# A wait on the previous group's landing ahead of each group's indirect returns

## The reference

```python
gates = softmax(xf @ router_w)
top_v, top_i = top_k(gates, 2)
masked = zeros_like(gates).at[arange(N)[:, None], top_i].set(top_v)
masked = masked / (masked.sum(-1, keepdims=True) + 1e-9)
# _ffn: h = x * rsqrt(mean(x*x) + eps) * rw; silu(h @ W1) @ W2   (128 -> 256 -> 128)
routed = vmap(lambda rw, W1, W2: _ffn(xf, rw, W1, W2))(rms_w, w1, w2)
routed_out = einsum('end,ne->nd', routed, masked)
return layernorm(x + routed_out + shared)
```

## Time and profile before

| | busy us | share of the span | instructions |
|---|---|---|---|
| TensorE matmul | 651.3 | 85% | 4299 |
| TensorE weight load | 554.7 | 72% | 4299 |
| VectorE | 596.1 | 77% | 1744 |
| ScalarE | 444.7 | 58% | 1225 |
| GpSimd | 501.3 | 65% | 545 |

### The profile page before, as it was taken

How to read it: one execution, slowest core, us unless ns; L and a number is a source line. 1 busy time by engine, 2 the same in 40 slices (tenths; PEclk the granted TensorE clock), 3 DMA queues, 4 the chain that set the end, 5 groups by cost and what they waited for, 6 DMA issues and landing times.

```text
span 769.2 us, 14716 instructions
## 1 busy us (share of the span) xinstructions
PE 651.3 (85%) x4299; PEld 554.7 (72%) x4299; DVE 596.1 (77%) x1744; ACT 444.7 (58%) x1225; POOL 501.3 (65%) x545
## 2 busy tenths in 40 slices
PE   5987798999999999999999997965988878767830
PEld 4765576788888888888888886854987768656720
DVE  4999999999999999999999864427447343698875
ACT  4885688867877876787787543411223111346445
POOL 1144565887797897888888776556655656566561
PEclk9999999999999999999999998878889889997865
DMA  8541111211221121111111055114222236536126
GB/s 305 193 138 42 43 43 41 64 57 55 62 64 62 60 62 50 63 64 60 59 50 62 22 167 192 45 55 101 80 80 77 76 80 172 168 100 205 60 80 218
DMA packets 62638, 70.76 MB, mean 92 GB/s; under 512 B 10335, under 2 KB 45285, under 8 KB 62304
## 3 DMA queue, kind: packets, MB, share of 16 engines
q1 hardware_dynamic: 41568, 47.70, 19.6%
q0 software_dynamic: 8608, 16.87, 6.5%
q10 hardware_dynamic: 12384, 5.26, 2.9%
HBM read 48.55 MB, written 23.01 MB: 93 GB/s over the span
## 4 chain that ended last, share of the span: by engine, by line
PE 60%; DVE 13%; issue 12%; ACT 7%; another core or an unknown queue 4%; ACTq 2%; DMA 1%; DVEq 0%; SPq 0%
PE bank L745 7%; PE bank L817 6%; PE bank L826 6%; PE bank L884 6%; PE bank L770 5%; PE bank L800 5%; DVE xbcT_area L1155 3%; PE bank L881 3%; PE bank L871 3%; PE bank L833 3%; PE bank L785 3%; PE bank L888 2%; DVE decay_area L1163 2%; ACT x L933 2%
## 5 line engine op out<-in xcount | busy, mean ns | idle before, releaser
L623 POOL DMA_INDIRECT returned<-xT,slots_in x141 | 142.1, 1008 | 107.6 <-DVE xT L1453 67.3
L669 POOL DMA_INDIRECT dispatched<-rows,row_u x128 | 143.7, 1123 | 33.9 <-issue 31.8
L745 PE MATMUL bank<-xT 128*128 128x128 f32 x564 | 92.0, 316 | 43.4 <-issue 24.9
L1155 DVE SCALAR_TENSOR_TENSOR xbcT_area<-raw,conv_w,xbcT_area 128x512 f32<-128x512 f32 x162 | 123.9, 766 | 2.9 <-ACT xbcT_area L999 2.9
L745 PEld LDWEIGHTS bank<-xT 128*128 128x128 f32 x564 | 82.7, 226 | 50.7 <-issue 42.4
L944 ACT ACTIVATE raw<-bank 128x512 f32<-128x512 f32 (+1 forms) x71 | 39.8, 590 | 126.9 <-remote 61.5
L661 POOL TENSOR_TENSOR state_kept<-state,whole 128x256 f32<-128x256 f32 x56 | 72.1, 1288 | 59.0 <-DVE state L1181 49.1
L1453 DVE COPY xT<-bank 128x512 f32<-128x512 f32 (+1 forms) x36 | 24.3, 676 | 90.5 <-remote 72.8
L770 PE MATMUL bank<-xbcT_area,raw 128*128 x564 | 83.4, 308 | 4.7 <-issue 4.6
L1163 DVE TENSOR_TENSOR_SCAN decay_area<-decay_area,ident_heads 128x512 f32<-128x512 f32 x64 | 85.0, 1329 | 0.0
L770 PEld LDWEIGHTS bank<-xbcT_area,raw 128*128 128x128 f32 x564 | 79.6, 224 | 7.0 <-issue 7.0
(11 more groups left out here) (228 smaller groups left out, 1497.0 us busy)
## 6 DMA issues: line engine op xcount, KB each, us to landing
decay_area<-decay_rows SPq DMA_DIRECT2D x64, 256.0 KB
slots_in<-dispatched ACTq DMA_DIRECT2D x77, 64.5 KB
hid<-returned SPq DMA_DIRECT2D x18, 256.0 KB
slots_in<-dispatched SPq DMA_DIRECT2D x64, 64.5 KB
xT<-xT_dram SPq DMA_DIRECT2D x8, 512.0 KB, 7.9
x<-x_dram SPq DMA_DIRECT2D x8, 512.0 KB, 7.8
out_dram<-x SPq DMA_DIRECT2D x16, 256.0 KB
xT<-returned SPq DMA_DIRECT2D x14, 256.0 KB
```

The costliest lines, as they stand in the source:

```text
L623: e.indirect_dma_start(returned, bass.IndirectOffsetOnAxis(ap=slots_in[sb_][:, n, D:ROW].bitcast(U32), axis=0), slots_out[b][:, n * P:(n + ...
L669: e.indirect_dma_start(dispatched, bass.IndirectOffsetOnAxis(ap=row_u[t % 2][:, m:m + 1], axis=0), rows[t % 3][:, k, c4, :], None).then_in ...
L745: mm = e.matmul(bank[:, off:off + P], w1_now[b][:, k * P:(k + 1) * P], slotsT[gr % len(slotsT)][:, n % 4 * P:(n % 4 + 1) * P], start=True, ...
L1155: e.scalar_tensor_tensor(o, r[:, n:n + W], conv_w[:, k, TAPS - 1 - n:TAPS - n], o, ALU.mult, ALU.add).then_inc(S["conv"])
```

## The change

In `return_rows`, GpSimd waits, for every group but the first, until the four returns of the group ahead of it have landed, before it issues its own. The group ahead has b = (gr - 1) % 3, and is the ((gr - 1) // 3 + 1)th to count on that semaphore. Nothing else is changed.

```diff
@@ -619,6 +619,8 @@
                 b, sb_ = gr % len(slots_out), gr % len(slots_in)
                 on.wait_ge("routed_out", gr + 1)
                 on.wait_ge(f"slots_in{sb_}", 16 * tiles_upto(gr, len(slots_in)))
+                if gr > 0:
+                    on.wait_ge(f"returned{(gr - 1) % len(slots_out)}", 64 * ((gr - 1) // len(slots_out) + 1))
                 for n in range(len(slot_tiles(gr))):
                     e.indirect_dma_start(returned, bass.IndirectOffsetOnAxis(ap=slots_in[sb_][:, n, D:ROW].bitcast(U32), axis=0),
                                          slots_out[b][:, n * P:(n + 1) * P], None, bounds_check=NOWHERE - 1,
```

## The result

The changed kernel takes 774.74 us (median of 4 runs, 772.85 to 776.12) where the kernel before takes 719.05. The ratio is 1.077, with a 95% interval of 1.074 to 1.080: 56 us slower. 748.6 us was predicted, in a range of 723 to 764. The direction and the mechanism were right, the size was not: 28 us of loss were forecast, half of what was measured.

What follows compares the result with a forecast made beforehand. In timed runs GpSimd's issue was taken to bound the middle, with each wait exposing a landing and a restart. Start of group 4 517.3, 31 periods of 6.82 us 211.4 and the end 19.9 gave 748.6 us, range 723 to 764.

Steps and rivals of the forecast that it cites:

- the sum: Changed kernel's timed run: group 4's start 517.3, 31 periods to group 35 211.4, the end 19.9; 748.6 us.
- the holds of TensorE: Routed part: TensorE's signals held about 5 us in the middle, 22.0 us together ahead of it; taken as absent in timed runs.
- the check of it: Kernel before, summed without the 22.0 us of holds: 517.3, 102, 75 and 19.9 give 714, near 720.5 us.
- The rival with real holds: Routed part: TensorE's holds occur in timed runs too, pace already near the floor; 722 to 734 us, chance 0.23.
- faster: Middle: the wait cuts runs of eight returns into fours and TensorE's hold goes; 709 us, chance 0.05.
- no effect: Returns: the wait never ends last, as the group ahead has always landed; 720 us, chance 0.04.
- groups 1 to 3 pay nothing: Ahead of the middle: groups 1 to 3 stand apart by far more than the gap, so the wait costs them nothing.
- The price of one wait: Between two groups on GpSimd: landing 1.25 plus restart 0.77, a gap of at least 2.02 us (1.9 to 2.4).
- TensorE's clock: Routed part: a slower middle may lower it further; priced at nothing, or a few us if VectorE's copy doesn't lead.
- a rival of 2.2 us throughout: Returns: landings of 2.2 us or more under load, period 7.8; 778 us, chance 0.06.
- The split between profile and timed runs: Span grows little, from 769.2 to 770 or 785, while timed runs grow by 28 us.
- Nothing behind GpSimd hides it: Routed part: three result buffers let VectorE run ahead, but what GpSimd can't issue is not made up for.

Runs made afterwards that it cites:

- the second profile: The kernel before, unchanged, profiled once more: 718.83 us, with a span of 717.1 us.
- the leaner TensorE: The kernel before with half of TensorE's products that make a group's result left out: 718.84 us, ratio 1.001.
- the first profile: The profile of the kernel before shown ahead of the prediction: a span of 769.2 us.
- a quarter of the picks' bytes: The changed kernel with only a quarter of the bytes of each of SyncE's picks fetched, same number of DMAs and waits: 766.59 us, ratio 1.067.
- the wait in the middle only: The kernel before with the wait of the change for groups 1 to 23 only: 756.62 us, ratio 1.053.
- the run with dead work: The kernel before with two dead GpSimd multiplications ahead of each group but the first, in place of the wait for a landing: 752.12 us, ratio 1.046.

## Why the prediction was right and wrong

**The step that failed** is the sum, 517.3 + 211.4 + 19.9, in two of its terms; the cost that it is built on, a landing and a restart in every group, was right. The start of group 4 was taken as 517.3 us, with nothing paid by groups 1 to 3, and is 526.66. The period was taken as 6.82 us for all 31 groups and is 7.36, most of it because some landings are slow.

**What bounds the kernel.** The reading that the holds of TensorE were absent in timed runs, and that GpSimd's issue is the pace there, was the step I was least sure of. It held: the second profile has no holds and 5.18 us per group for groups 4 to 24 (5.12 was used), and the leaner TensorE changed nothing. That the check of it came to 714, near the measured 720.5, was partly luck: its start of group 4 was 6.0 us too low, and its last stretch, 75 us, 4.1 too high. The rival with real holds (722 to 734) is out, as are "faster" and "no effect".

**The start of group 4.** I took 517.3 us, the first profile's 539.31 less the two holds. It is 523.29 in the kernel before and 526.66 in the changed one, 9.4 us later than used. The first 6.0 of these: I took out TensorE's holds and didn't ask what is late next. It is GpSimd itself, which has eight dispatches between groups 1 and 2 and eight between 3 and 4, at 1.27 us each, on the same queue. In the second profile they run up to the first return of group 4; the first row is the first return of group 3:

```profile
507.74 0.98 POOL L623 DMA_INDIRECT returned<-xT,slots_in  x1 [0.30 <-issue]
...
522.03 0.96 POOL L669 DMA_INDIRECT dispatched<-rows,row_u  x1 [0.30 <-DVE xT L1453]
523.29 0.98 POOL L623 DMA_INDIRECT returned<-xT,slots_in  x1 [0.30 <-issue]
```

The other 3.4: "groups 1 to 3 pay nothing". Group 1 and group 3 each pay 1.8 us. I had read their distance from copies that were held up in the first profile; without the holds these copies were ready (group 3's at 499.93, its first return at 511.22).

**The price of one wait** was right in kind and 0.10 us low: 2.12 us between groups instead of 2.02, the landing 1.27 us (1.25 used) and the restart 0.85 (0.77 used, taken from a wait for another engine's semaphore). 31 times 0.10 are 3.1 us. TensorE's clock, feared to add to it, went from 0.97 and 0.91 to 0.87 and 0.89 in the two stretches from 545 to 660 us and is not on the chain.

**Slow landings** were the term that was mis-sized. I took one landing for all 31 groups and kept a uniform 1.7 us as the upper bound, with a rival of 2.2 us throughout at 0.06. The real form is neither: 23 of the 31 gaps are 2.00 to 2.15 us; seven in the middle are longer, by 6.5 us in all, and one behind them, by 3.5. Those ahead of groups 21, 22, 23 and 29, 7.7 of these 10 us, stand where the picks run, traffic that had been in the trace; with a quarter of the picks' bytes 5.8 us of them are gone. The cause of the other four, 2.3 us, is open. Another 2.3 come from a pause inside group 32, whose four returns take 7.15 us instead of 4.80; it is in the kernel before too (6.90), so it belongs to the sum and not to the loss. Some 1 comes from lesser ones. Together with the 3.1: 16.6 us, the 228.0 us measured less the 211.4 of the sum.

The two terms, 9.4 and 16.6, are the 26 us between 748.6 and 774.7. The end of 19.9 us was 19.0, and the median of the timed runs is 1.0 above the profiled span.

**The loss, stretch by stretch.** A right total for the changed kernel isn't a right loss, so the same terms are laid against the kernel before. Up to group 4 nothing was forecast, and 3.4 us were lost. From 4 to 24 it was 20 x (6.82 - 5.12) = 34 us, and 41.8 were lost. From 24 to 35 it was 11 x (6.82 - 6.81), nothing, and 11.8 were lost: VectorE's 6.81 us per group was read from the profile with the holds, where the second profile has 6.44, and 7.52 were needed. That is the largest miss of a stretch. The forecast loss of 28 us is 34 less the 6 by which the sum for the kernel before fell short of its measured time.

**The split between profile and timed runs** was forecast as a test: the span to grow little, the timed runs by 28. The span grew by 4.5 us and the timed runs by 56. The test spoke for the right case, but it compared an execution with holds with one without.

**What hides a delay.** "Nothing behind GpSimd hides it" was right with the wait in all groups and is wrong with the wait in the middle only: there GpSimd is 41 us behind at group 24 (667.88 against 626.83), and the span ends 35 us later (751.9 against 717.1).

## What to carry to other kernels

Where one engine issues transfers back to back and is the pace of a stretch, a wait for its own last landing costs landing plus restart less the usual gap, each time: here 2.12 - 0.30 = 1.8 us, and more where other transfers fill the DMA engines. Where another engine is the pace by a small margin only, it costs too: 11.8 us over the 11 groups behind group 24. The same wait one step further back is free. When the profiled execution is much longer than the timed ones, take a second profile before trusting any wait in the first, and when a wait is taken out of the sum, walk each queue to see which one is late next.

## What was not expected of the hardware

- The same kernel gave profiles of 769.2 and 717.1 us. In the first, copies stood up to 12 us behind TensorE's products (group 4's: 525.72 to 537.82); no other profile here shows this, and its cause stays open.
- A landing took 1.27 us after the last issue of four had ended, and 1.12 behind group 35's only one. With the DMA engines' share at 1.05 it took 4.1 us, at 1.08 4.8 us.
- GpSimd's next DMA started 0.85 us after the landing that it waited for, and a lone DMA with its wait took 3.1 us where one in a row takes 1.28.
- A multiplication of 128x256 took GpSimd 0.64 us in the run with dead work and 1.0 us on average in the main loop (line 614). VectorE's load alone doesn't explain it: at a busy share of 93% (660 to 730 us of that run) the dead ones still took 0.64 to 0.66 us in the median. The cause stays open.
